# Split matmul operands of a fused graph block as pairs of float16 instead of 32-bit words

## The chip, the cores and the metric

The kernel runs on one core of one Trainium2 chip. The metric is the device time of one execution in microseconds (us); lower is better. TensorE does matmuls and transposes (the profile calls it PE, and its weight loads PEld), VectorE is DVE, ScalarE is ACT, GpSimd is POOL, and SP starts most of the DMAs.

## The reference

128 graphs of 128 nodes with 256 features each go through two stages. Stage L0 is a transformer block with 8 heads of 32 features and an adjacency bias; stage L1 is two rounds of single-head graph attention.

```python
# L0, for x of (128, 128, 256)
nx = ln(x); q, k, v = nx @ wq + bq, nx @ wk + bk, nx @ wv + bv       # 8 heads of 32
bias = where(adj > 0, 0.1 * adj * adj, -inf)
attn = softmax(q @ k.T / sqrt(32) + bias);  x1 = x + (attn @ v) @ wo + bo
x = x1 + gelu(ln(x1) @ w1 + b1) @ w2 + b2                             # 256 -> 1024 -> 256
# L1, for k in 0, 1
q, kk = x @ Wq[k].T + bq[k], x @ Wk[k].T + bk[k]                      # 256 -> 128
attn = softmax(where(adj == 0, -1e10, q @ kk.T / sqrt(128)))          # zero where masked
x = ln(x + (attn @ x) @ Wc[k].T) * g[k] + b[k]
```

## The kernel before

The 128 graphs are worked in 32 groups of 4, so that a group has 512 rows. All weights stay in SBUF. A matmul with a weight matrix needs more precision than one pass gives, so both operands are split in a high part (`_h`) and a low part (`_l`, the rest), and `mm3` makes three matmuls of one: high by high, high by low, low by high. Those are lines 244, 245 and 246 of the profile. The high part is made by ScalarE (it copies with a cast), the low part by VectorE (it subtracts the high part), and for the odd chunks of the hidden layer by GpSimd.

In this kernel the halves of the weights and of `xT`, `rot`, `hid` and `cT` (the transposed rows of each stage) are tiles of type float32r, 32-bit words that a matmul takes in one pass. The halves of q and k, of the softmax of L0 (`pT16`) and of v are float16 already. `to_columns` multiplies with a weight as the stationary operand and 512 rows as the moving one (128x512); `to_rows` and the `down` matmuls have 128 rows as the stationary operand and a weight of 256 columns as the moving one (128x256). Transposes, and the L1 scores and value products, are plain float32 and not part of the change.

Five lists of steps (`TENSOR`, `SCALAR`, `VECTOR`, `GPSIMD`, `SYNC`), written by hand, give the order of each engine's work in the steady loop; a step such as `M.down5-2` is chunk 5 of the second MLP product, two groups behind. Each engine does its list in order and waits by semaphores. One pass through the lists is one group. The step names that the prediction uses: `Q.k1` (a projection of L0), `C0.xW` (x times Wc in L1's first round, evicted by ScalarE to `cW`, then needed by `C0.PT` and `C0.PV`), `M.mT` and `M.up0` (transposes and first chunk of the MLP), `M.lo6` (low part of hidden chunk 6, on VectorE, from `split_hidden`, line 251), `C0.S`, `C1.S` (scores of L1).

The names of the profile are without digits: `w_h` is `w1_h` or `w2_h`, `area` is the scratch that holds scores, x1, x2, `cW` and the hidden layer.

Of the kernel before, what the change touches and what calls it, by code (L numbers as in the profile page):

```python
# [29 lines left out]
F32, F32R, F16, BF16, I32 = (mybir.dt.float32, mybir.dt.float32r, mybir.dt.float16,  # L30
                             mybir.dt.bfloat16, mybir.dt.int32)
ALU, ACT, AX = mybir.AluOpType, mybir.ActivationFunctionType, mybir.AxisListType

P = 128
# [12 lines left out]
RING = 3  # L47

# [28 lines left out]
def graph_blocks(nc, x, adj, ln1_g, ln1_b, ln2_g, ln2_b, wq, bq, wk, bk, wv, bv, wo, bo, w1, b1,  # L77
# [6 lines left out]
    with ExitStack() as ctx:  # L84
        def sb(name, shape, dt=F32):
            return ctx.enter_context(nc.sbuf_tensor(name, shape, dt))
# [7 lines left out]
        wqk_h, wqk_l = sb("wqk_h", [P, KC, 2 * D], F32R), sb("wqk_l", [P, KC, 2 * D], F32R)  # L94
        wv_h, wv_l = sb("wv_h", [P, KC, D], F32R), sb("wv_l", [P, KC, D], F32R)
        wo_h, wo_l = sb("wo_h", [P, KC, D], F32R), sb("wo_l", [P, KC, D], F32R)
        w1_h, w1_l = sb("w1_h", [P, KC, FF], F32R), sb("w1_l", [P, KC, FF], F32R)
        w2_h, w2_l = sb("w2_h", [P, FC, D], F32R), sb("w2_l", [P, FC, D], F32R)
        cqk_h, cqk_l = sb("cqk_h", [P, L, KC, 2 * P], F32R), sb("cqk_l", [P, L, KC, 2 * P], F32R)
        cw_h, cw_l = sb("cw_h", [P, L, KC, D], F32R), sb("cw_l", [P, L, KC, D], F32R)  # L100
# [6 lines left out]
        ln_q = sb("ln_q", [P, KC])  # L107
        cln_col = sb("cln_col", [P, 2, KC])
        cgq = sb("cgq", [P, KC])
# [22 lines left out]
        xT_h, xT_l = sb("xT_h", [P, KC, R], F32R), sb("xT_l", [P, KC, R], F32R)  # L132
# [6 lines left out]
        rot_h, rot_l = sb("rot_h", [P, KC, R], F32R), sb("rot_l", [P, KC, R], F32R)  # L139
        hid_h, hid_l = sb("hid_h", [P, RING, R], F32R), sb("hid_l", [P, RING, R], F32R)  # L140
        cT_h, cT_l = sb("cT_h", [P, KC, R], F32R), sb("cT_l", [P, KC, R], F32R)
# [227 lines left out]
        def _(pool):  # L369
# [3 lines left out]
            pool.memset(v_h[:, :, :, HD:VW], 1.0).then_inc(const_ok, 1)  # L373
# [75 lines left out]
        def _(act):  # L449

            act.wait_ge(prep_dve, 1)
# [14 lines left out]
            def iteration(it, odd):  # L466
                for stage, what, g in steps(SCALAR, it, odd):
# [79 lines left out]
        def _(dve):  # L547
            made = [0]

            def prep(instruction):  # L550
                made[0] += 1
                instruction.then_inc(prep_dve, 1)
# [4 lines left out]
            def lows(start, stop):  # L557

                for n in range(start, stop):
# [7 lines left out]
                    prep(dve.scalar_tensor_tensor(lo, raw, gain, hi.bitcast(F32), ALU.mult, ALU.subtract))  # L567
# [23 lines left out]
            prep(dve.tensor_scalar(ln_q[:, :], ln_col[:, 0, :], QSCALE, None, ALU.mult))  # L591
# [3 lines left out]
            prep(dve.tensor_scalar(cgq[:, :], cln_col[:, 0, :], CSCALE, None, ALU.mult))  # L595
# [29 lines left out]
            def iteration(it, odd):  # L625
                for stage, what, g in steps(VECTOR, it, odd):
                    b = int(what[-1]) if what[-1].isdigit() else None
                    if what == "mA":
# [7 lines left out]
                        dve.scalar_tensor_tensor(adj_f, adj_in[:, :, :], 0.1, adj_in[:, :, :],  # L636
# [16 lines left out]
                    elif stage == "N":  # L653
                        need(dve, a_xT, g, 1, 1)
                        dve.tensor_tensor(xT_l[:, :, :], psC, xT_h[:, :, :].bitcast(F32), ALU.subtract)\
# [21 lines left out]
                    elif stage == "A" and what[:3] == "max":  # L677
# [3 lines left out]
                        dve.tensor_scalar(nbias[:, b, :], nmax[:, b, :], -1.0, P_SCALE,  # L681
# [15 lines left out]
                    elif what == "oT":  # L697
                        need(dve, a_oT, g, 1, 1)
                        dve.tensor_tensor(rot_l[:, :, :], psA, rot_h[:, :, :].bitcast(F32), ALU.subtract)\
                           .then_inc(d_oT, 1)  # L700
                    elif what == "wo":
# [3 lines left out]
                        dve.tensor_tensor(x1, psA_rows, xin[:, g[1]], ALU.add).then_inc(d_x1, 1)  # L705
# [5 lines left out]
                    elif what == "mT":  # L711
                        need(dve, a_mT, g, 1, 1)
                        dve.tensor_tensor(rot_l[:, :, :], psM, rot_h[:, :, :].bitcast(F32), ALU.subtract)\  # L713
# [3 lines left out]
                    elif what == "x2":  # L717
# [424 lines left out]
```

## Time and profile before

| | us |
|---|---|
| median of three runs | 2311.23 |
| lowest, highest | 2309.97, 2317.95 |
| the profiled execution | 2311.21 |
| its span, first to last instruction | 2309.4 |

A row of the grouped view gives the line, engine and operation, what is written and read with the shapes, the number of instructions, then the busy time in us and the mean of one in ns, then the idle time of the engine just before them. A timeline row gives the start and the length in us. Matmuls are pipelined: the length of one is longer than its place in the stream, and the pace of a stream is the distance from one start to the next.

### The profile page before, as it was taken

What the parts mean: (1) busy time and instruction counts of PE and PEld (TensorE: products, weight loads), DVE (VectorE), ACT (ScalarE), POOL (GpSimd) and SP (SyncE); (2) the same over time, 40 slices, a digit from 0 to 9 for tenths busy, and PEclk for the clock granted to TensorE, in tenths of its full rate; (3) what the DMA queues carried; (4) which work ended last, traced back from release to release, by engine and by line L of the source; (5) the groups of instructions that cost most, each with busy time, mean ns of one, the idle gap of its engine ahead of it and who ended that gap; (6) DMA issues with size and microseconds to landing.
All of it is one profiled execution on the core that took longest, in us unless ns stands there. A gap on an engine that the chain in (4) does not pass through costs nothing.

```text
span 2309.4 us, 47435 instructions
## 1 busy us (share of the span) xinstructions
PE 2112.8 (91%) x16984; PEld 1898.2 (82%) x16984; DVE 1837.9 (80%) x3585; ACT 1566.9 (68%) x2994; POOL 874.1 (38%) x632
## 2 busy tenths in 40 slices
PE   5589999999999999999999999999999999999863
PEld 4578888888888888888888888898888888888752
DVE  3566788888888888888888888888888888887433
ACT  2367777777768776776787677777767777787421
POOL 2021343334444433343444333444433344444423
PEclk8799999999999999999999999999999999999985
DMA  3321112122221121222111122221111222210000
GB/s 100 71 53 34 39 36 51 47 56 56 56 57 42 29 53 45 56 56 56 46 39 42 42 56 56 56 56 43 35 49 43 56 56 55 56 47 15 15 10 18
DMA packets 103649, 108.61 MB, mean 47 GB/s; under 512 B 9824, under 2 KB 78432, under 8 KB 103456
## 3 DMA queue, kind: packets, MB, share of 16 engines
q1 hardware_dynamic: 102912, 104.90, 18.0%
q8 instruction: 163, 2.67, 0.5%
q0 software_dynamic: 544, 0.80, 0.2%
q14 instruction: 30, 0.25, 0.0%
HBM read 38.55 MB, written 16.78 MB: 24 GB/s over the span
## 4 chain that ended last, share of the span: by engine, by line
PE 76%; ACT 10%; DVE 9%; issue 3%; POOL 1%; DMA 0%; SPq 0%; POOLq 0%; DVEq 0%; ACTq 0%
PE ps L244 20%; PE ps L246 19%; PE ps L245 19%; PE ps L1114 5%; PE ps L816 5%; PE ps L1040 4%; PE ps L1094 3%; DVE hid_l L251 2%; ACT cs L530 2%; DVE rot_l L713 2%; ACT L530 2%; ACT area L538 1%; PE ps L1033 1%; ACT rot_h L502 1%; ACT ck L524 1%
## 5 line engine op out<-in xcount | busy, mean ns | idle before, releaser
L251 POOL TENSOR_TENSOR hid_l<-area,hid_h 128x512 fp32r<-128x512 f32 x128 | 165.4, 1292 | 721.2 <-ACT hid_h L512 721.2
L489 ACT ACTIVATE area<-area,nbias 128x128 f32<-128x128 f32 x1024 | 313.9, 392 | 1.0 <-DVE nbias L681 0.2
L244 PE MATMUL ps<-w_h,hid_h 128*128 128x256 f32 x1024 | 305.3, 298 | 3.2 <-POOL hid_l L251 1.8
L245 PE MATMUL ps<-w_l,hid_h 128*128 128x256 f32 x1024 | 286.2, 279 | 0.0
L246 PE MATMUL ps<-w_h,hid_l 128*128 128x256 f32 x1024 | 285.9, 279 | 0.0
L509 ACT ACTIVATE area<-ps,b_col 128x512 f32<-128x512 f32 x256 | 176.3, 689 | 118.3 <-PE ps L246 117.2
L244 PE MATMUL ps<-rot_h,w_h 128*128 128x512 f32 x512 | 215.3, 420 | 11.6 <-DVE rot_l L713 10.8
L674 DVE TENSOR_TENSOR area<-ps,biasA 128x1024 f32<-128x1024 f32 x128 | 155.8, 1218 | 79.4 <-PE ps L1033 77.6
L246 PE MATMUL ps<-rot_h,w_l 128*128 128x512 f32 x512 | 202.2, 395 | 0.0
L245 PE MATMUL ps<-rot_l,w_h 128*128 128x512 f32 x512 | 202.0, 395 | 0.0
L244 PEld LDWEIGHTS ps<-w_h,hid_h 128*128 128x128 f32 x1024 | 193.1, 189 | 7.9 <-POOL hid_l L251 2.2
L245 PEld LDWEIGHTS ps<-w_l,hid_h 128*128 128x128 f32 x1024 | 194.0, 189 | 3.7
L246 PEld LDWEIGHTS ps<-w_h,hid_l 128*128 128x128 f32 x1024 | 193.0, 188 | 0.0
L403 POOL TENSOR_TENSOR ve<-mv,eps_cols 128x4 f32<-128x4 f32 x128 | 26.9, 210 | 422.5 <-DVE mv L577 421.8
L524 ACT ACTIVATE cq<-ps,cb_col 128x512 f32<-128x512 f32 x64 | 43.9, 686 | 206.9 <-PE ps L246 206.9
L512 ACT CAST hid_h<-area 128x512 fp32r<-128x512 f32 x256 | 159.1, 621 | 8.1
L685 DVE TENSOR_TENSOR pT<-ps,pT 128x1024 f16<-128x1024 f32 x128 | 155.6, 1216 | 11.1 <-ACT pT L495 9.5
L415 POOL TENSOR_TENSOR x<-x,cb_row 128x1024 f32<-128x1024 f32 x64 | 161.8, 2527 | 5.0
L426 POOL TENSOR_TENSOR area<-area,cwb_row 128x1024 f32<-128x1024 f32 x32 | 76.3, 2383 | 221.8 <-ACT area L538 221.8
L679 DVE TENSOR_REDUCE nmax<-area 128x8 f32<-128x1024 f32 x128 | 155.4, 1214 | 1.1
L816 PE MATMUL ps<-ident,area 128*128 128x128 f32 x1024 | 135.4, 276 | 21.4 <-DVE area L585 18.7
L244 PE MATMUL ps<-cw_h,cT_h 128*128 128x256 f32 x512 | 146.9, 287 | 5.5 <-DVE cs L733 5.5
(176 smaller groups left out, 6952.3 us busy)
## 6 DMA issues: line engine op xcount, KB each, us to landing
qkS<-qk SPq DMA_DIRECT2D x384, 128.0 KB, 2.4
xin<-in_x SPq DMA_DIRECT2D x32, 512.0 KB, 4.0
adj_in<-in_adj SPq DMA_DIRECT2D x64, 256.0 KB, 4.0
out<-x SPq DMA_DIRECT2D x32, 512.0 KB, 3.3
area<-in_L_gnn_w SPq DMA_DIRECT2D x2, 1024.0 KB, 11.9
area<-in_L_gnn_Wc SPq DMA_DIRECT2D x2, 256.0 KB, 11.9
area<-in_L_gnn_wq SPq DMA_DIRECT2D x1, 256.0 KB, 3.5
area<-in_L_gnn_wk SPq DMA_DIRECT2D x1, 256.0 KB, 4.4
```

Source lines behind the costliest of these rows:

```text
L244: pe.matmul(dst, lh, rh, start=start, stop=False, **kw)
L245: pe.matmul(dst, lh, rl, start=False, stop=False, **kw)
L246: return pe.matmul(dst, ll, rh, start=False, stop=stop, **kw)
L251: eng.tensor_tensor(hid_l[:, c % RING, :], hidden[:, c % 2, :], hid_h[:, c % RING, :].bitcast(F32), ALU.subtract).then_inc(done, 1)
L415: pool.tensor_tensor(dst, dst, over_graphs(cb_row[:, l, :]), ALU.add).then_inc(p_c[l], 1)
L489: last = act.activation(sc[:, b % 2, h], sc[:, b % 2, h], ACT.Exp, bias=nbias[:, b, h:h + 1])
L509: act.activation(hidden[:, b % 2, :], psUp, ACT.Gelu, bias=b1_col[:, b:b + 1]).then_inc(a_gelu, 1)
L512: act.copy(hid_h[:, b % RING, :], hidden[:, b % 2, :]).then_inc(a_hi, 1)
L674: dve.tensor_tensor(sc[:, b % 2], psA_heads, biasA[:, b].unsqueeze(1).broadcast_to([P, H, P]), ALU.add).then_inc(d_S, 1)
L679: dve.tensor_reduce(nmax[:, b, :], sc[:, b % 2], AX.X, ALU.max).then_inc(d_max, 1)
L685: dve.tensor_tensor(pT16[:, b % 2, 1], psA_heads, pT16[:, b % 2, 0], ALU.subtract)\
L816: last = pe.transpose(dst[:, c, b * P:(b + 1) * P], rows[:, b, c * P:(c + 1) * P], ident[:, :])
```

## The change

All split tiles become float16. High parts are then rounded to float16, low parts are the float16 of what is left. So that the low parts of weights don't fall below the range of float16, weights are multiplied by 256 when they are split, and the places that read a product from PSUM divide by 256 (q and k of L0 stay scaled; their scores are divided by 65536 inside the exponential, and the bias is multiplied by it). The ones column of v, from which the sum of the softmax comes, is 256 too, so that the division by it removes the factor of v.

```diff
-        w2_h, w2_l = sb("w2_h", [P, FC, D], F32R), sb("w2_l", [P, FC, D], F32R)
+        w2_h, w2_l = sb("w2_h", [P, FC, D], F16), sb("w2_l", [P, FC, D], F16)
...                       (wqk, wv, wo, w1, cqk, cw, xT, rot, hid, cT alike)
-            pool.memset(v_h[:, :, :, HD:VW], 1.0).then_inc(const_ok, 1)
+            pool.memset(v_h[:, :, :, HD:VW], W_SCALE).then_inc(const_ok, 1)
...
-            act.wait_ge(prep_dve, 1)
+            act.wait_ge(prep_dve, 3)
...
                             last = act.activation(sc[:, b % 2, h], sc[:, b % 2, h], ACT.Exp,
-                                                  bias=nbias[:, b, h:h + 1])
+                                                  bias=nbias[:, b, h:h + 1], scale=1.0 / QK_SCALE)
...
                         act.activation(hidden[:, b % 2, :], psUp, ACT.Gelu,
-                                       bias=b1_col[:, b:b + 1]).then_inc(a_gelu, 1)
+                                       bias=b1_col[:, b:b + 1], scale=1.0 / W_SCALE).then_inc(a_gelu, 1)
...
                             act.activation((cq, ck)[i][:, :], psC[:, i, :], ACT.Identity,
-                                           bias=cb_col[:, i, l:l + 1]).then_inc((a_cq, a_ck)[i][l], 1)
+                                           bias=cb_col[:, i, l:l + 1],
+                                           scale=1.0 / W_SCALE).then_inc((a_cq, a_ck)[i][l], 1)
...
-                            act.copy(cW, psC_rows).then_inc(a_cW[l], 1)
+                            act.activation(cW, psC_rows, ACT.Copy, scale=1.0 / W_SCALE).then_inc(a_cW[l], 1)
...
-            prep(dve.tensor_scalar(ln_q[:, :], ln_col[:, 0, :], QSCALE, None, ALU.mult))
+            prep(dve.tensor_scalar(ln_q[:, :], ln_col[:, 0, :], QSCALE * W_SCALE, None, ALU.mult))
+            prep(dve.tensor_scalar(ln_kv[:, 0, :], ln_col[:, 0, :], W_SCALE, None, ALU.mult))
+            prep(dve.tensor_scalar(ln_kv[:, 1, :], ln_col[:, 2, :], W_SCALE, None, ALU.mult))
...
-                        dve.tensor_scalar(nbias[:, b, :], nmax[:, b, :], -1.0, P_SCALE,
+                        dve.tensor_scalar(nbias[:, b, :], nmax[:, b, :], -1.0 / QK_SCALE, P_SCALE,
...
-                        dve.tensor_tensor(x1, psA_rows, xin[:, g[1]], ALU.add).then_inc(d_x1, 1)
+                        dve.scalar_tensor_tensor(x1, psA_rows, 1.0 / W_SCALE, xin[:, g[1]],
+                                                 ALU.mult, ALU.add).then_inc(d_x1, 1)
...
-                        dve.tensor_tensor(x2, psM_rows, x1, ALU.add).then_inc(d_x2, 1)
+                        dve.scalar_tensor_tensor(x2, psM_rows, 1.0 / W_SCALE, x1,
+                                                 ALU.mult, ALU.add).then_inc(d_x2, 1)
```

Four small VectorE instructions are added in the preparation ahead of the first group. In the loop no instruction is added, removed or moved on any engine: the sequences are the same, and in 64 places each a `COPY` of ScalarE (`cW`) becomes an `ACTIVATE`, and a `TENSOR_TENSOR` of VectorE (`x1`, `x2`) a `SCALAR_TENSOR_TENSOR`. No DMA changes, since the weights are still loaded as float32 and split on the chip.

## Rows read from the trace of the kernel before

**Rows 1.** The page: busy time by engine; granted TensorE clock, tenths, 40 slices

```profile
PE 2112.8 (91%) x16984; PEld 1898.2 (82%) x16984; DVE 1837.9 (80%) x3585; ACT 1566.9 (68%) x2994; POOL 874.1 (38%) x632
...
PEclk8799999999999999999999999999999999999985
```

**Rows 2.** A stretch: length, PE, PEld, DVE, ACT, POOL busy, clock, DMA share, GB/s

```profile
948.00:1596.00 648.00, 623.99 (x5093) 563.80 (x5093) 557.33 (x1091) 472.47 (x902) 262.78 (x187) 1.00 0.19 47
```

**Rows 3.** Waits of PE from 300 to 2100: us in total, times, longest

```profile
PE ps L244 <- issue: 16.5, 10, 2.0
PE ps L1105 <- ACT area L538: 14.6, 28, 0.6
PE ps L1094 <- ACT ck L524: 11.0, 27, 0.4
PE ps L244 <- DVE qk L660: 9.0, 13, 0.9
```

**Rows 4.** Timeline, DVE: start, length; the same step of two successive groups

```profile
1181.59 1.22 DVE L674 TENSOR_TENSOR area<-ps,biasA 128x1024 f32<-128x1024 f32 x1 [3.10 <-PE ps L1033]
...
1247.49 1.23 DVE L674 TENSOR_TENSOR area<-ps,biasA 128x1024 f32<-128x1024 f32 x1 [1.39 <-PE ps L1033]
```

**Rows 5.** The chain that ended last, from 300 to 2100, shares by line

```profile
by line: PE ps L244 21.8%; PE ps L246 20.6%; PE ps L245 20.5%; PE ps L816 5.3%; PE ps L1114 5.3%; PE ps L1040 4.1%; PE ps L1094 3.0%; DVE hid_l L251 2.6%; issue 2.4%; ACT cs L530 2.2%; ACT L530 2.0%; DVE rot_l L713 1.9%; ACT rot_h L502 1.4%
```

**Rows 6.** Timeline, PE: three streams of 24 matmuls, first of each and what follows

```profile
1186.50 0.40 PE L244 MATMUL ps<-rot_h,w_h 128*128 128x512 f32 x1
...
1192.09 1.05 PE L1094 MATMUL ps<-ck,cq 128*128 128x128 f32 x8
...
1215.35 0.28 PE L244 MATMUL ps<-wo_h,rot_h 128*128 128x256 f32 x1
...
1218.17 0.40 PE L244 MATMUL ps<-cT_h,cqk_h 128*128 128x512 f32 x1
...
1224.31 0.28 PE L244 MATMUL ps<-cw_h,cT_h 128*128 128x256 f32 x1
...
1227.03 1.04 PE L816 MATMUL ps<-ident,area 128*128 128x128 f32 x8
```

**Rows 7.** Timeline, PE: eight float16 matmuls, then a float32r product starts

```profile
1246.83 0.62 PE L1033 MATMUL ps<-qkS 96*128 96x128 f16 x8
1247.26 0.48 PE L244 MATMUL ps<-rot_h,w_h 128*128 128x512 f32 x1
1247.58 0.40 PE L245 MATMUL ps<-rot_l,w_h 128*128 128x512 f32 x1
```

**Rows 8.** Groups by line and form: matmuls of two products (first of three each)

```profile
L244 PE MATMUL ps<-w_h,hid_h 128*128 128x256 f32 x1024 | 305.3, 298 | 3.2 <-POOL hid_l L251 1.8 <-DVE hid_l L251 1.3
...
L244 PE MATMUL ps<-rot_h,w_h 128*128 128x512 f32 x512 | 215.3, 420 | 11.6 <-DVE rot_l L713 10.8 <-ACT area L509 0.8
```

**Rows 9.** Groups by line and form: weight loads of 32-bit and of float16 operands

```profile
L246 PEld LDWEIGHTS ps<-w_h,hid_l 128*128 128x128 f32 x1024 | 193.0, 188 | 0.0
...
L246 PEld LDWEIGHTS ps<-v_h,pT 128*128 128x128 f16 x1024 | 79.6, 96 | 0.0
```

**Rows 10.** Groups by form: a PSUM tile read in two ways on ACT and DVE

```profile
L478 ACT ACTIVATE qk<-ps,bqk_col 128x512 f16<-128x512 f32 x128 | 88.0, 687 | 40.0 <-PE ps L246 39.7
...
L483 ACT CAST v_h<-ps 128x512 f16<-128x512 f32 x64 | 37.2, 581 | 116.7 <-PE ps L246 116.7
...
L660 DVE SCALAR_TENSOR_TENSOR qk<-ps,bqk_col,qk 128x512 f16<-128x512 f32 x128 | 95.4, 745 | 51.0 <-ACT qk L478 51.0
...
L665 DVE TENSOR_TENSOR v_l<-ps,v_h 128x512 f16<-128x512 f32 x64 | 42.9, 671 | 0.0
```

**Rows 11.** Low parts of the hidden layer on VectorE: the group, then one (timeline)

```profile
L251 DVE TENSOR_TENSOR hid_l<-area,hid_h 128x512 fp32r<-128x512 f32 x128 | 121.5, 949 | 19.3 <-ACT hid_h L512 19.3
...
1200.48 2.30 DVE L251 TENSOR_TENSOR hid_l<-area,hid_h 128x512 fp32r<-128x512 f32 x1
```

**Rows 12.** Timeline, POOL, the same time

```profile
1199.85 2.38 POOL L413 TENSOR_TENSOR x<-xh,cg_row 128x1024 f32<-128x1024 f32 x1 [1.73 <-DMA out<-x]
```

More of the change, by code:

```diff
@@ L28 @@
 from concourse import mybir
-F32, F32R, F16, BF16, I32 = (mybir.dt.float32, mybir.dt.float32r, mybir.dt.float16,
-                             mybir.dt.bfloat16, mybir.dt.int32)
+F32, F16, BF16, I32 = mybir.dt.float32, mybir.dt.float16, mybir.dt.bfloat16, mybir.dt.int32
 ALU, ACT, AX = mybir.AluOpType, mybir.ActivationFunctionType, mybir.AxisListType
@@ L47 @@
 RING = 3
+W_SCALE = 256.0
+QK_SCALE = W_SCALE * W_SCALE
 TENSOR = ["Q.k0+0", "M.down2-2", "A.S2-1", "M.up4-2", "C0.q-3", "A.PT1-1", "M.down3-2", "M.up5-2",
@@ L92, in graph_blocks @@
         ident = sb("ident", [P, P])
[L94 to L97, printed above, removed]
-        w2_h, w2_l = sb("w2_h", [P, FC, D], F32R), sb("w2_l", [P, FC, D], F32R)
-        cqk_h, cqk_l = sb("cqk_h", [P, L, KC, 2 * P], F32R), sb("cqk_l", [P, L, KC, 2 * P], F32R)
-        cw_h, cw_l = sb("cw_h", [P, L, KC, D], F32R), sb("cw_l", [P, L, KC, D], F32R)
+        wqk_h, wqk_l = sb("wqk_h", [P, KC, 2 * D], F16), sb("wqk_l", [P, KC, 2 * D], F16)
+        wv_h, wv_l = sb("wv_h", [P, KC, D], F16), sb("wv_l", [P, KC, D], F16)
+        wo_h, wo_l = sb("wo_h", [P, KC, D], F16), sb("wo_l", [P, KC, D], F16)
+        w1_h, w1_l = sb("w1_h", [P, KC, FF], F16), sb("w1_l", [P, KC, FF], F16)
+        w2_h, w2_l = sb("w2_h", [P, FC, D], F16), sb("w2_l", [P, FC, D], F16)
+        cqk_h, cqk_l = sb("cqk_h", [P, L, KC, 2 * P], F16), sb("cqk_l", [P, L, KC, 2 * P], F16)
+        cw_h, cw_l = sb("cw_h", [P, L, KC, D], F16), sb("cw_l", [P, L, KC, D], F16)
         ln_col = sb("ln_col", [P, 4, KC])
@@ L106, in graph_blocks @@
         cb_col = sb("cb_col", [P, 2, L])
-        ln_q = sb("ln_q", [P, KC])
+        ln_q, ln_kv = sb("ln_q", [P, KC]), sb("ln_kv", [P, 2, KC])
         cln_col = sb("cln_col", [P, 2, KC])
-        cgq = sb("cgq", [P, KC])
+        cgq, cgk = sb("cgq", [P, KC]), sb("cgk", [P, KC])
         bo_row, b2_row = sb("bo_row", [P, D]), sb("b2_row", [P, D])
@@ L131, in graph_blocks @@
         xin = sb("xin", [P, 2, B, D])
[L132 removed]
+        xT_h, xT_l = sb("xT_h", [P, KC, R], F16), sb("xT_l", [P, KC, R], F16)
         qk16 = sb("qk16", [P, 4, 2, R], F16)
@@ L138, in graph_blocks @@
         v_h, v_l = sb("v_h", [P, B, H, VW], F16), sb("v_l", [P, B, H, VW], F16)
-        rot_h, rot_l = sb("rot_h", [P, KC, R], F32R), sb("rot_l", [P, KC, R], F32R)
-        hid_h, hid_l = sb("hid_h", [P, RING, R], F32R), sb("hid_l", [P, RING, R], F32R)
-        cT_h, cT_l = sb("cT_h", [P, KC, R], F32R), sb("cT_l", [P, KC, R], F32R)
+        rot_h, rot_l = sb("rot_h", [P, KC, R], F16), sb("rot_l", [P, KC, R], F16)
+        hid_h, hid_l = sb("hid_h", [P, RING, R], F16), sb("hid_l", [P, RING, R], F16)
+        cT_h, cT_l = sb("cT_h", [P, KC, R], F16), sb("cT_l", [P, KC, R], F16)
         cq, ck = sb("cq", [P, R]), sb("ck", [P, R])
@@ L287, in graph_blocks @@
             halves += [(wqk_h[:, c, 0:D], wqk_l[:, c, 0:D], raw_qkvo[:, 0, c], ln_q[:, c:c + 1]),
-                       (wqk_h[:, c, D:2 * D], wqk_l[:, c, D:2 * D], raw_qkvo[:, 1, c], ln_col[:, 0, c:c + 1]),
-                       (wv_h[:, c], wv_l[:, c], raw_qkvo[:, 2, c], ln_col[:, 0, c:c + 1])]
-        halves += [(wo_h[:, :, :], wo_l[:, :, :], raw_qkvo[:, 3], 1.0)]
+                       (wqk_h[:, c, D:2 * D], wqk_l[:, c, D:2 * D], raw_qkvo[:, 1, c], ln_kv[:, 0, c:c + 1]),
+                       (wv_h[:, c], wv_l[:, c], raw_qkvo[:, 2, c], ln_kv[:, 0, c:c + 1])]
+        halves += [(wo_h[:, :, :], wo_l[:, :, :], raw_qkvo[:, 3], W_SCALE)]
         HALVES_QKVO = len(halves)
         for c in range(KC):
-            halves += [(w1_h[:, c], w1_l[:, c], raw_w1[:, c], ln_col[:, 2, c:c + 1])]
+            halves += [(w1_h[:, c], w1_l[:, c], raw_w1[:, c], ln_kv[:, 1, c:c + 1])]
         HALVES_W1 = len(halves)
-        halves += [(cqk_h[:, 0, :, 0:P], cqk_l[:, 0, :, 0:P], layer_qk[0][:, 0], CSCALE),
-                   (cqk_h[:, 0, :, P:2 * P], cqk_l[:, 0, :, P:2 * P], layer_qk[0][:, 1], 1.0),
-                   (cw_h[:, 0], cw_l[:, 0], layer_w[0], 1.0)]
+        halves += [(cqk_h[:, 0, :, 0:P], cqk_l[:, 0, :, 0:P], layer_qk[0][:, 0], CSCALE * W_SCALE),
+                   (cqk_h[:, 0, :, P:2 * P], cqk_l[:, 0, :, P:2 * P], layer_qk[0][:, 1], W_SCALE),
+                   (cw_h[:, 0], cw_l[:, 0], layer_w[0], W_SCALE)]
         HALVES_C0 = len(halves)
         for c in range(KC):
-            gain = cln_col[:, 0, c:c + 1]
+            gain = cgk[:, c:c + 1]
             halves += [(cqk_h[:, 1, c, 0:P], cqk_l[:, 1, c, 0:P], layer_qk[1][:, 0, c], cgq[:, c:c + 1]),
@@ L304, in graph_blocks @@
         HALVES_L1 = len(halves)
-        halves += [(w2_h[:, :, :], w2_l[:, :, :], raw_w2, 1.0)]
-        PREP_DVE = 14 + len(halves)
-        BV_MADE = 1 + HALVES_W1 + 6
+        halves += [(w2_h[:, :, :], w2_l[:, :, :], raw_w2, W_SCALE)]
+        PREP_DVE = 18 + len(halves)
+        BV_MADE = 3 + HALVES_W1 + 8
         L1_COPIED = BV_MADE + 3
@@ L566, in lows @@
                     dve.wait_ge(prep_act, made)
-                    prep(dve.scalar_tensor_tensor(lo, raw, gain, hi.bitcast(F32), ALU.mult, ALU.subtract))
+                    prep(dve.scalar_tensor_tensor(lo, raw, gain, hi, ALU.mult, ALU.subtract))
             def stats(g, n, rows):
@@ L600, in _ @@
             prepped()
-            prep(dve.tensor_scalar(bqk_col[:, 0:2], bqk_col[:, 0:2], QSCALE, None, ALU.mult))
+            prep(dve.tensor_scalar(bqk_col[:, 0:2], bqk_col[:, 0:2], QSCALE * W_SCALE, None, ALU.mult))
+            prep(dve.tensor_scalar(bqk_col[:, 2:4], bqk_col[:, 2:4], W_SCALE, None, ALU.mult))
             prep(dve.tensor_copy(bv_rep, bv_col[:, :].unsqueeze(2).broadcast_to([P, KC, P])))
-            assert made[0] == BV_MADE
+            assert made[0] == BV_MADE, made[0]
             dve.wait_ge(prep_pe, 2)
@@ L698, in iteration @@
                         need(dve, a_oT, g, 1, 1)
-                        dve.tensor_tensor(rot_l[:, :, :], psA, rot_h[:, :, :].bitcast(F32), ALU.subtract)\
+                        dve.tensor_tensor(rot_l[:, :, :], psA, rot_h[:, :, :], ALU.subtract)\
                            .then_inc(d_oT, 1)
@@ L712, in iteration @@
                         need(dve, a_mT, g, 1, 1)
-                        dve.tensor_tensor(rot_l[:, :, :], psM, rot_h[:, :, :].bitcast(F32), ALU.subtract)\
+                        dve.tensor_tensor(rot_l[:, :, :], psM, rot_h[:, :, :], ALU.subtract)\
                            .then_inc(d_mT, 1)
```

11 lines of the change are left out of this document (6 added, 5 removed).

## The prediction

> **What bounds the kernel now.** I read the page first. PE is busy 91% of the span and DVE 80% [rows 1]; the length of one matmul overlaps the next, so 91% doesn't yet say that PE is the bound. A stretch of the steady loop has PE busy 624 of 648 us and DVE 557, at the full clock of 2.4 GHz [rows 2]. The waits say the rest: from 300 to 2100 us PE waits at four places for the sum of 51 us, 3% [rows 3], and everything else is its own stream. The same step of two successive groups starts 65.9 us apart [rows 4]: that is the period, and 32 groups with the filling and the draining make the span. The chain of that stretch is 62.9% on lines 244 to 246, the three matmuls of a split product, another 18% on other PE lines, and some 19% on ACT, DVE and issue [rows 5]. So PE's pace sets the time, but not alone: a fifth of the chain is latency of the engines that evict and split.
>
> **The pace of a split matmul.** A stream's pace is start to start. Twenty-four float32r matmuls of 512 columns take 5.59 us, 233 ns each; 24 of `wo` with 256 columns take 2.82 us, 117.5 ns; 24 of `cw` take 2.72 us, 113.3 ns [rows 6]. Eight float16 matmuls of 128 columns take 0.43 us, 54 ns each [rows 7]. At 2.4 GHz one column per cycle would be 213, 107 and 53 ns. So the float16 stream runs at about a column per cycle and the float32r ones 6 to 10% slower, at two sizes in proportion, which looks like a cost per column and not per instruction. What I take for float16: 216 ns and 108 ns, four times and twice the 54 of rows 7. The saving is 17, 9.5 and 5.3 ns. Bounds: nothing, if the slow pace comes from adding into PSUM, which the eight of rows 7 do not do; and at most 20, 11 and 7 ns, down to a column per cycle.
>
> Per group there are 96 matmuls of 512 columns (a third of each line's 512 plus 256 plus 256 over 32 groups: `rot` with w1 512 [rows 8], and `xT` and `cT` 256 each by the code), 120 of 256 columns in `down` and `wo` (1024 [rows 8] and 256 per line), and 72 in `xW` and `v` (512 and 256 per line). That is 96 x 17 + 120 x 9.5 + 72 x 5.3 ns = 1.63 + 1.14 + 0.38 = 3.15 us.
>
> **The weight load at the start of a run.** A load takes 188 ns with 32-bit words and 96 ns with float16 [rows 9]. Within a stream it hides under the matmul before; after a short one it can't. The first float32r matmul behind the eight float16 ones holds the stream 0.32 us instead of 0.23 [rows 7], while those eight, which follow a float32r product themselves, show no such excess in their mean of 54. The list `TENSOR` goes from another kind of matmul into a split product 14 times per group. At 0.09 us, less the shorter load, all 14 would give 1.2 us; a few start behind a wait, where some of it is hidden, so I take 0.9 us. Zero is not possible here unless a float16 load of these tiles is slower than that of `pT`.
>
> The Trainium skill (TensorE: Matmul & The Clock Gate, Weight-path perf modes) has a fast weight load for 128 columns of a type that is not FP32, which agrees with 96 against 188. The same section says that the array takes one element per cell and cycle whatever the element's width: by that rule the 3.15 us would be nothing, and only the 0.9 left. The rows speak against it, since 233 is not four times 54; it is the second rival.
>
> **What the edits cost.** `cW` goes from a copy to an activation. On a PSUM tile of 512 columns an activation takes 687 ns and a cast 581 [rows 10]: 0.1 us more, twice per group. One of the two, `C0.xW`, is what PE waits for at L1105 in each group (28 times [rows 3]): 32 x 0.106 = 3.4 us on the path. The other feeds GpSimd's `cWb`, with no wait of PE behind it in rows 3: nothing. `x1` and `x2` become three-operand instructions: 745 against 671 ns [rows 10], 0.07 us twice per group at most, 4.7 us in all. DVE has 14% idle [rows 2] which hides part; queued behind `x1` are the statistics, for which `M.mT` waits. I take 1.5 us. The exponential, gelu and q and k change a constant only. A cast that writes float16 costs what one into float32r does as far as rows go: nothing. The four small instructions of the preparation run while weights are still on their way. GpSimd's subtraction with a float16 input has no row; nothing is what I take, and up to some tenths of a us stay hidden unless PE waits for its chunk, which it doesn't in rows 3. Sum of costs: 5 us.
>
> **What arrives at the end.** PE's own work falls by 3.15 + 0.9 = 4.05 us a group, 130 us over 32 groups, 5.6%. Not all of it can show:
> - The split matmuls are 96 x 0.233 + 120 x 0.1175 + 72 x 0.113 + 1.2 = 45.8 us of 65.9, 69% of the time. On the chain the three lines have 62.9%; about 4% of it are the float16 products of v, between 96 x 14 ns and 96 x 54 ns by columns or by instruction from rows 7. So 59 of 69 parts are on the chain: 130 x 0.85 = 111 us.
> - Where PE waits for ACT or DVE, their latency doesn't shrink, and PE now comes earlier. The order of the lists is fixed for the old durations, and DVE is busy 86% of the steady loop [rows 2]; with 4 us less it would be 92%. Late next, after the four places of rows 3, are the low parts that PE needs soonest: `rot_l` and `hid_l` (1.9% and 2.6% of the chain already [rows 5]). I choose to give a quarter of the rest to such new waits: 83 us.
> - The first 300 and last 200 us are latency more than stream (the granted clock is 8 and 7 tenths in the first two slices and 5 in the last [rows 1]); some 5 us go there. That leaves 78.
>
> 78 less 5 is 73 us: 2311.2 (the profiled execution, which is the median within 0.1 us) less 73 is 2238.
>
> **Rivals.**
> 1. *Nothing is lost.* ACT and DVE move forward with PE, because most of their idle time is waiting for PE. Then 130 less 5: 2186. For it: DVE's 86% of 65.9 us [rows 2, 4] are 57 us, still under a period of 62. Against: the 19% of other engines on the chain. Between this and the forecast lies a continuum; I take it as up to 2205. Chance 0.13.
> 2. *Width doesn't set the pace*; the 6 to 10% come from the accumulation or another cause that float16 keeps. Then 0.9 us x 32 = 29, of which 85% and three quarters remain, 18, less 5: 2298. Chance 0.17.
> 3. *The other engines take it all*: the loop through DVE's in-order list is already nearly as long as PE's, so the new waits eat nearly everything: 2300 to 2315. Against it: PE waits 3% only, so what it waits for is mostly early. Chance 0.07.
> 4. *Slower, by a collision.* One `hid_l` of VectorE per group takes 2.30 us where the mean is 949 ns and the rest 0.7 [rows 11]; at that time GpSimd runs an addition of 2.38 us [rows 12], and the two instructions with two SBUF inputs seem not to run together. There are four such `hid_l` a group. If the shorter times shift more of them under GpSimd's long ones, each costs 1.6 us x 32 = 51 us of DVE and, at the head of a `down`, of PE. One more eats two thirds of the gain, two more turn it: 2238 + 102 = 2340. Nothing shows that the shift, some 4 us over a period, would pick the wrong direction; one that leaves would be a gain. Chance 0.05.
>
> The rest, 0.58, is the forecast with 2205 to 2290 as its own range.
>
> **How the numbers follow.** A difference under 0.5% (12 us) can't be told from none here. Faster by more is the forecast, the first rival, and most of the second where it reaches below 2299.7 (0.6 of 0.17), together 0.83. Same: the rest of the second and most of the third, 0.11. Slower: 0.06, from the fourth and a little of the third. The range reaches from the first rival's near half to the second's middle: 2192 to 2298.
>
> **What the profile after would show.** Streams of 512 columns with starts 216 ns apart and of 256 with 108 (the second rival: still 233 and 113 to 118). Weight loads of all split products at 96 ns; the step behind the eight score matmuls at 0.23 or less instead of 0.32. The period under 65.9 us, near 63.7. PE waits at L1105, L1094, `rot_l` and `Q.k1` longer than the 51 us of now, by 20 to 40 us. `cW` on ACT at 1.1 us. The forecast would be wrong by the pace (an unshown type at these sizes), or by how many waits come through, which I set by judgement; the sign would be wrong only by a lengthened DVE, which the mean of its `hid_l` would tell.

## The result, and the profile after

The changed kernel takes 2274.38 us (2272.66 to 2277.72, four runs), the kernel before 2310.6 us (2309.05 to 2317.95, four runs) on the same chip: a ratio of 0.9849, 95% interval 0.9828 to 0.987. The gain is 36 us where 73 were forecast. The time lies inside the range of 2192 to 2298, but half of the expected gain is missing, so the working of the prediction has a step that failed, and the question of the experiments is which. The profiled execution took 2277.72 us with a span of 2275.9.

The page after: busy time by engine, and the chain that ended last by engine.

```profile
PE 2026.2 (89%) x16984; PEld 1512.2 (66%) x16984; DVE 1887.3 (83%) x3589; ACT 1562.6 (69%) x2994; POOL 845.8 (37%) x632
...
PE 56%; DVE 21%; ACT 13%; issue 7%; POOL 1%; DMA 0%; SPq 0%; DVEq 0%; POOLq 0%; ACTq 0%
```

Against [rows 1] PE's busy time falls by 87 us and that of its weight loads by 386 us. VectorE's *rises* by 49 us, although its instructions are the same but for 64 and four small ones. That is the first thing to explain. The window of 648 us (columns as in [rows 2]) says the same of the steady loop: VectorE goes from 557 to 575 us, and PE drops to 608 of 648, so it now waits for longer.

```profile
948.00:1596.00 648.00, 607.59 (x5215) 456.65 (x5213) 575.41 (x1092) 480.15 (x920) 260.02 (x188) 0.99 0.19 49
```

The waits of PE from 300 to 2100, after:

```profile
PE ps L245 <- DVE qk L666: 47.8, 27, 2.3
PE ps L245 <- issue: 19.4, 10, 2.2
PE ps L1113 <- ACT area L540: 17.1, 27, 0.7
PE ps L1102 <- ACT ck L525: 11.4, 27, 0.4
PE ps L245 <- DVE rot_l L720: 7.6, 27, 0.3
```

In [rows 3] four places sum to 51 us, and with the 6.3 us for `rot_l`, which is the next in that view, to 57; the same five sum to 103 here. Of these 46 us more, 39 are at one place, `Q.k1`, which waits for q or k of VectorE (9.0 before, 47.8 now).

The pace of PE's streams, by the same reading as [rows 6]:

```profile
1171.33 0.38 PE L245 MATMUL ps<-rot_h,w_h 128*128 128x512 f16 x1
...
1176.51 1.05 PE L1102 MATMUL ps<-ck,cq 128*128 128x128 f32 x8
...
1178.71 0.61 PE L1041 MATMUL ps<-qkS 96*128 96x128 f16 x8
1179.16 0.27 PE L245 MATMUL ps<-cw_h,cT_h 128*128 128x256 f16 x1
1179.27 0.27 PE L246 MATMUL ps<-cw_l,cT_h 128*128 128x256 f16 x1
...
1181.78 0.38 PE L245 MATMUL ps<-xT_h,wqk_h 128*128 128x512 f16 x1
```

Twenty-four matmuls of 512 columns take 5.18 us, 216 ns each instead of 233; 24 of `cw` take 2.62 us, 109 ns instead of 113.3. Note that the length of one (0.38, 0.27) says nothing of the pace. From the first of the eight score matmuls to the first of `cw`, and on to the second, it is 0.45 + 0.11 us; the same entry takes 0.43 + 0.20 in the kernel before (medians of 27 groups).

Last, what VectorE and GpSimd do when PE waits at `Q.k1` (three timelines: VectorE, PE, GpSimd).

```profile
1179.14 1.18 DVE L746 TENSOR_SCALAR cmax<-cneg 128x4 f32<-128x4 f32 x1
...
1184.54 2.47 DVE L252 TENSOR_TENSOR hid_l<-area,hid_h 128x512 f16<-128x512 f32 x1
1186.93 0.74 DVE L666 SCALAR_TENSOR_TENSOR qk<-ps,bqk_col,qk 128x512 f16<-128x512 f32 x1
```

```profile
1187.73 0.39 PE L245 MATMUL ps<-xT_h,wqk_h 128*128 128x512 f16 x1 [1.07 <-DVE qk L666]
```

```profile
1177.93 2.36 POOL L416 TENSOR_TENSOR x<-x,cb_row 128x1024 f32<-128x1024 f32 x1
...
1184.10 2.36 POOL L414 TENSOR_TENSOR x<-xh,cg_row 128x1024 f32<-128x1024 f32 x1 [1.50 <-DMA out<-x]
```

`hid_l` starts 0.44 us after a GpSimd multiplication and ends 0.55 us after that one's end at 1186.46. This `hid_l` is the step `M.lo6`. VectorE's part of the eviction of q (`Q.q1`, L666) is queued behind it and begins only then, and PE's next projection behind that. `cmax`, an instruction over 4 elements per partition, takes 1.18 us and ends at 1180.32, when GpSimd's addition ends (1180.29).

The groups of VectorE in which its time grew, and the weight load; after, then before (the row of `hid_l` of before is in [rows 11], of the load in [rows 9]).

```profile
L252 DVE TENSOR_TENSOR hid_l<-area,hid_h 128x512 f16<-128x512 f32 x128 | 137.7, 1076 | 21.7 <-ACT hid_h L513 20.5
L587 DVE TENSOR_SCALAR xh<-xh,mv,rs 128x256 f32<-128x256 f32 x128 | 67.4, 589 | 0.7 <-POOL rs L406 0.7
L746 DVE TENSOR_SCALAR cmax<-cneg 128x4 f32<-128x4 f32 x64 | 60.1, 939 | 2.2
L687 DVE TENSOR_SCALAR nbias<-nmax 128x8 f32<-128x8 f32 x128 | 45.0, 351 | 4.4
L247 PEld LDWEIGHTS ps<-w_h,hid_l 128*128 128x128 f16 x1024 | 100.1, 98 | 11.6
```

```profile
L585 DVE TENSOR_SCALAR xh<-xh,mv,rs 128x256 f32<-128x256 f32 x128 | 52.1, 470 | 0.7 <-POOL rs L405 0.7
L738 DVE TENSOR_SCALAR cmax<-cneg 128x4 f32<-128x4 f32 x64 | 37.5, 585 | 2.2
L681 DVE TENSOR_SCALAR nbias<-nmax 128x8 f32<-128x8 f32 x128 | 31.7, 247 | 4.4
```

The excess is 127 ns x 128 + 119 x 128 + 354 x 64 + 104 x 128 = 67 us, 2.1 us per group. Nothing in these four but the types of `hid_l`'s operands and the factor of `nbias` was changed.

The collision itself is not new. Only one `hid_l` of the four in a group is stretched, in both kernels: `M.lo6` takes over 1.5 us in 27 of its 32 groups before and in 28 after, and its mean goes from 1.74 to 2.25 us, while the other three stay at 0.68 to 0.69. So `M.lo6` doesn't stand under GpSimd's pass more often now, it meets it earlier and stands there longer.

### The profile page after: what moved, and what is told of

Its sections match the earlier page's. It is cut to its first block, busy times and chain, and to the rows that moved or that the text cites. A ratio compares the mean times of both kernels' runs of the same rounds, so it can differ in the third digit from the quotient of the medians.

```text
span 2275.9 us, 47439 instructions
## 1 busy us (share of the span) xinstructions
PE 2026.2 (89%) x16984; PEld 1512.2 (66%) x16984; DVE 1887.3 (83%) x3589; ACT 1562.6 (69%) x2994; POOL 845.8 (37%) x632
## 4 chain that ended last, share of the span: by engine, by line
PE 56%; DVE 21%; ACT 13%; issue 7%; POOL 1%; DMA 0%; SPq 0%; DVEq 0%; POOLq 0%; ACTq 0%
PE ps L245 13%; PE ps L247 13%; PE ps L246 13%; PE ps L824 5%; PE ps L1122 5%; PE ps L1048 3%; DVE hid_l L252 3%; DVE nmax L685 3%; ACT area L490 3%; DVE xh L587 2%; PE ps L1102 2%; DVE rot_l L720 2%; DVE qk L666 2%; DVE st L574 1%; ACT L490 1%
## 5 line engine op out<-in xcount | busy, mean ns | idle before, releaser
L252 POOL TENSOR_TENSOR hid_l<-area,hid_h 128x512 f16<-128x512 f32 x128 | 148.7, 1162 | 748.7 <-ACT hid_h L513 748.7
L245 PE MATMUL ps<-w_h,hid_h 128*128 128x256 f16 x1024 | 279.0, 272 | 2.7 <-DVE hid_l L252 1.6
L247 PE MATMUL ps<-w_h,hid_l 128*128 128x256 f16 x1024 | 279.1, 273 | 0.0
L246 PE MATMUL ps<-w_l,hid_h 128*128 128x256 f16 x1024 | 279.1, 273 | 0.0
L680 DVE TENSOR_TENSOR area<-ps,biasA 128x1024 f32<-128x1024 f32 x128 | 155.6, 1216 | 66.1 <-PE ps L1041 66.0
L245 PE MATMUL ps<-rot_h,w_h 128*128 128x512 f16 x512 | 195.0, 381 | 12.7 <-DVE rot_l L720 11.2
L246 PE MATMUL ps<-rot_l,w_h 128*128 128x512 f16 x512 | 194.7, 380 | 0.0
L247 PE MATMUL ps<-rot_h,w_l 128*128 128x512 f16 x512 | 194.7, 380 | 0.0
L513 ACT CAST hid_h<-area 128x512 f16<-128x512 f32 x256 | 158.3, 618 | 8.2
L824 PE MATMUL ps<-ident,area 128*128 128x128 f32 x1024 | 136.7, 277 | 21.9 <-DVE area L587 19.1
L252 DVE TENSOR_TENSOR hid_l<-area,hid_h 128x512 f16<-128x512 f32 x128 | 137.7, 1076 | 21.7 <-ACT hid_h L513 20.5
L1048 PE MATMUL ps<-ident,area 128*128 128x128 f32 x1024 | 138.5, 280 | 11.3 <-ACT area L490 7.0
L245 PE MATMUL ps<-cw_h,cT_h 128*128 128x256 f16 x512 | 141.0, 275 | 6.1 <-DVE cs L741 6.1
```

The costliest lines, as they stand in the source:

```text
L245: pe.matmul(dst, lh, rh, start=start, stop=False, **kw)
L246: pe.matmul(dst, lh, rl, start=False, stop=False, **kw)
L247: return pe.matmul(dst, ll, rh, start=False, stop=stop, **kw)
L680: dve.tensor_tensor(sc[:, b % 2], psA_heads, biasA[:, b].unsqueeze(1).broadcast_to([P, H, P]), ALU.add).then_inc(d_S, 1)
L824: last = pe.transpose(dst[:, c, b * P:(b + 1) * P], rows[:, b, c * P:(c + 1) * P], ident[:, :])
L1048: last = pe.transpose(psA_heads[:, h], sc[:, b % 2, h], ident[:, :])
```

## The experiments

Theory A: the pace and nothing else gives the gain, about 94 us from the streams above, and the rest of it is eaten because VectorE's instructions from SBUF to SBUF now stand longer under GpSimd's 2.4 us instructions. Theory B: the gain is lost to latency that doesn't shrink, as the prediction had it, or to the edits themselves. Eleven kernels ran, named by what they change. Beside them the kernel before was measured again, with medians of 2310.2 to 2311.6 us, so that their times can be set against the two above.

**1 and 2. A light GpSimd, in both kernels.** The passes that multiply by the gain, add the bias, and add b2 to x1 work on 16 of 256 columns; the same in the changed kernel (first) and in the kernel before (second). Everything else stays in place and order; what these passes would do to the other 240 columns is left out.

```diff
-pool.tensor_tensor(dst, src, over_graphs(cg_row[:, l, :]), ALU.mult).then_inc(p_cg[l], 1)
+pool.tensor_tensor(dst[:, :, 0:16], src[:, :, 0:16], over_graphs(cg_row[:, l, :])[:, :, 0:16], ALU.mult).then_inc(p_cg[l], 1)
...                 (the addition of cb_row, and that of b2_row to x1, alike)
```

> The changed kernel, but GpSimd's two affine passes after each norm of L1 and its addition to x1 work on 16 columns of a graph's 256 instead of all (the outputs lack the gain and bias of the rest). Theory A (the gain was eaten because VectorE instructions on SBUF operands now stand under GpSimd's 2.4 us passes: hid_l 1076 ns mean, cmax 939, xh 589): these go back to 0.69, 0.17 and 0.41 us, and the time falls from 2274 to about 2225. Rival B (the port is innocent; the fixed latency of ScalarE and VectorE in order holds the period): 2262 to 2274.

> The same cut of GpSimd's passes in the kernel before. Theory A: its collisions cost less (hid_l 949 ns, cmax 585), so 2311 falls to about 2290, and the ratio of the two light kernels is 0.970 to 0.975, near what was forecast, instead of 0.985. Rival B: 2300 to 2311 and a ratio still 0.985.

Measured: 2195.99 us (0.9499, 0.9474 to 0.9524) with the change, 2283.35 us (0.9871, 0.9845 to 0.9897) without. Between these two the change is worth 87 us, a ratio of 0.962, where it is worth 36 in the full kernels. Both times are lower than either expectation had them (about 2225 and 2290, ratio 0.970 to 0.975). The light kernel also drains sooner, which is part of that: behind the last step of L1's bias (`biasC`) on VectorE 87 us are left instead of 99 without the change, and 81 instead of 95 with it; in the pair this cancels to 2 us. What is left of the effect of GpSimd's passes on the loop is 27 - 12 = 15 us in the kernel before and 78 - 14 = 64 us in the changed one. The light changed kernel, window, waits and groups:

```profile
948.00:1596.00 648.00, 624.41 (x5402) 470.64 (x5401) 558.18 (x1130) 495.96 (x959) 160.58 (x196) 1.00 0.19 51
```

```profile
PE ps L245 <- issue: 19.0, 10, 2.2
PE ps L1113 <- ACT area L540: 17.4, 28, 0.7
PE ps L1102 <- ACT ck L525: 12.2, 28, 0.9
PE ps L245 <- DVE rot_l L720: 9.1, 28, 1.6
```

```profile
L252 DVE TENSOR_TENSOR hid_l<-area,hid_h 128x512 f16<-128x512 f32 x128 | 87.4, 683 | 22.4 <-ACT hid_h L513 21.4
...
L746 DVE TENSOR_SCALAR cmax<-cneg 128x4 f32<-128x4 f32 x64 | 11.3, 177 | 2.2
```

and the group of the light kernel before:

```profile
L251 DVE TENSOR_TENSOR hid_l<-area,hid_h 128x512 fp32r<-128x512 f32 x128 | 87.4, 683 | 18.1 <-ACT hid_h L512 18.1
```

Writing float16 costs `hid_l` nothing (683 ns in both), `cmax` takes 177 ns, and the wait at `Q.k1` is gone. The waits that stay are 58 us here, and 65 with the small ones that the view lists below these; the light kernel before has 49 and 50 by the same count. So A holds, and of the latency that the prediction feared, 15 us in 1800 are to be seen. Light passes also end sooner, which could help whoever waits for GpSimd; the next experiments leave them at full length.

**3 and 4. One step of VectorE later, in both kernels.** `M.lo6` changes places with the q eviction that PE waited for behind it.

```diff
-"A.AV0-1", "M.lo6-2", "Q.q1+0",
+"A.AV0-1", "Q.q1+0", "M.lo6-2",
```

> The changed kernel with two neighbours of VectorE's list exchanged: the subtraction of Q.q1 ahead of M.lo6, which needs nothing of it. Theory A: PE's wait at Q.k1 for that subtraction (1.8 us per group, behind a hid_l of 2.5 us) disappears, 2274 becomes about 2235. Rival B (the wait only moves to the next low part or softmax step): above 2265.

> The same exchange in the kernel before, where the wait is 0.3 us per group. Theory A: 2311 falls by 5 to 12 us. Rival B: no change within 3 us. With e3 it tells whether the changed kernel alone is bound there.

Measured: 2239.56 us (0.9684, 0.966 to 0.9708) after, 2296.68 us (0.9933, 0.9904 to 0.9962) before. The swap gives 35 us with the change, 4 short of the first expectation, and 14 without, a little over the 5 to 12 expected; the pair is 57 us apart. The wait behind q is gone, but another, as the second expectation had it, stands in its place, for the softmax that is queued behind `M.lo6` now:

```profile
PE ps L1048 <- DVE pT L691: 15.6, 17, 1.0
```

**5. The factors alone.** The scaled kernel with all tiles left as 32-bit words.

```diff
-        w2_h, w2_l = sb("w2_h", [P, FC, D], F16), sb("w2_l", [P, FC, D], F16)
+        w2_h, w2_l = sb("w2_h", [P, FC, D], F32R), sb("w2_l", [P, FC, D], F32R)
...                 (all split tiles alike; the factors stay)
```

> Only the other half of the change: weights times 256, the evictions and the softmax with their factors, cW by an activation, x1 and x2 by three-operand instructions, but all split tiles still float32r. Theory A (the profile after has cW at 1007 ns for 998 and x1, x2 at 1225 for 1225): no change, 2308 to 2316 beside 2311. Rival B (my 5 us of costs): 2316 or more.

Measured: 2311.84 us against 2310.53, ratio 1.0002 (0.9986 to 1.0018). Groups of that kernel: `cW` on ScalarE, then x2 and x1 on VectorE.

```profile
L541 ACT ACTIVATE area<-ps 128x1024 f32<-128x1024 f32 x64 | 64.6, 1010 | 6.0 <-PE ps L248 6.0
...
L729 DVE SCALAR_TENSOR_TENSOR area<-ps,area 128x1024 f32<-128x1024 f32 x32 | 39.2, 1225 | 4.7 <-PE ps L248 0.5
L712 DVE SCALAR_TENSOR_TENSOR area<-ps,xin 128x1024 f32<-128x1024 f32 x32 | 39.2, 1224 | 17.2 <-PE ps L248 17.2
```

The copy took 998 ns in the kernel before, and x1 as a plain addition 1224. In sum the edits cost nothing that can be measured, and the whole change of time comes with the type of the operands. The sum hides two shifts. With the factors, products on 32-bit words run slower: summed start to start over 24 groups they take 0.7 us per group more (one of `cw` 119 ns instead of 113, medians), though nothing in these matmuls but the values and the place of the tiles differs. And PE's waits from 300 to 2100 us are 46 us instead of 58. Why is open; the float16 streams, with the same factors, run at 109 ns.

**6 and 10. The type of some products alone,** with the light GpSimd so that no collision blurs it: only `hid` and w2 (the `down` matmuls) as float16; then only `rot`, w1 and wo.

```diff
-        w2_h, w2_l = sb("w2_h", [P, FC, D], F32R), sb("w2_l", [P, FC, D], F32R)
+        w2_h, w2_l = sb("w2_h", [P, FC, D], F16), sb("w2_l", [P, FC, D], F16)
...                 (hid_h, hid_l alike; in the other kernel rot, w1 and wo instead)
```

> GpSimd's passes light as in the light kernels, scaling as in the change, and float16 only for the hidden layer and w2 (the down product, 96 matmuls of 256 columns per group, entered six times from another kind of matmul); the rest stays float32r (outputs lack gain and bias as before). Beside 2283 of the light kernel with words. Theory A (only the pace pays, an entry pays only behind a float16 block, which down has once per group): 0.8 to 0.9 us per group, 2255 to 2260. Rival B (each of the entries pays 0.075 us, as the prediction counted): 1.25 us per group, 2240 to 2246.

> As e6, but float16 for rot, w1 and wo only (48 matmuls of 512 columns and 24 of 256 per group), beside 2283 of the light kernel with words. Theory A (the pace alone: 48 x 17 + 24 x 8.5 ns = 1.0 us per group): 2248 to 2254. Rival B (entries pay as the prediction counted): 2235 to 2242.

Measured: 2263.19 us (0.98, 0.9768 to 0.9832) for `down`, 2262.1 us (0.979, 0.9773 to 0.9808) for `rot`, w1 and wo; against the light kernel before 20 us and 21 us. By pace alone I would work out 96 x 8.4 ns x 32 = 26 us and (48 x 17.1 + 24 x 8.4) ns x 32 = 33 us. Both expectations on the first asked for more than was found, the one with a gain at the start of each run above all. On the second both expected a larger gain than the 21 us. The remaining products then hold 87 - 41 = 46 us, where the pace gives 36.

The parts can't be read so finely, because the light kernel before has no factors and these two have: the products that stay on words run slower here too. Summed start to start over 24 groups they take 0.6 us per group more in the first of the two and 1.2 us in the second than in the light kernel before, 19 and 39 us in 32 groups. That is more than the 6 and 12 us that are missing; shorter waits and other steps give part of it back. So these two kernels neither confirm nor refute the pace of a single product, and by themselves they don't refute the gain at the starts either; the entries are read from the traces below.

**7 and 8. The low part later still, in both kernels.** `M.lo6` goes behind the softmax and value steps too.

```diff
-"A.AV0-1", "M.lo6-2", "Q.q1+0", "A.PT2-1", "A.AV1-1", "Q.k1+0"
+"A.AV0-1", "Q.q1+0", "A.PT2-1", "A.AV1-1", "M.lo6-2", "Q.k1+0"
```

> The changed kernel with M.lo6 later in VectorE's list: behind A.AV1, where VectorE waits anyway, and where GpSimd's second pass of C0.af is nearly over; the subtraction of Q.q1 and the softmax step A.PT2 go ahead of it. Theory A (VectorE's list ahead of Q.k1 holds the period, and hid_l costs 2.5 us only beside that pass): both the wait and the collision go, 2205 to 2225. Rival B (the wait of PE moves to the low part itself or to PT3): 2235 or above, as the simple exchange gave.

> The same move in the kernel before. Theory A: 2285 to 2295, since its wait there was 0.3 us per group. Ratio of the two late kernels 0.965 to 0.972, near that of the light pair (0.962). Rival B: ratio 0.975 or above, as for the simple exchange.

Measured: 2221.05 us (0.9604, 0.9588 to 0.962) after, 2292.88 us (0.9913, 0.9895 to 0.993) before. This is a full kernel and the fastest of the full ones: 90 us under the kernel before and 53 under the changed one. The same move gives 18 us without the change. The pair is 72 us apart. Its `hid_l` and `cmax`:

```profile
L252 DVE TENSOR_TENSOR hid_l<-area,hid_h 128x512 f16<-128x512 f32 x128 | 101.1, 790 | 21.8 <-ACT hid_h L513 20.2
...
L746 DVE TENSOR_SCALAR cmax<-cneg 128x4 f32<-128x4 f32 x64 | 60.1, 938 | 2.2
```

`hid_l` is down from 1076 ns, `cmax` is as long as in the changed kernel, and no wait of PE in the view is put down to it: a stretched instruction matters where PE's next operand is queued behind it. Both times are as the first expectation had them, the ratio of the pair too (0.969). Of the 25 us that this kernel is behind the light one, 14 are draining; the other 11 are in no wait that the view lists.

**9. One GpSimd pass light.** Only the gain and bias of `C0.af`, the pass under which `M.lo6` stands, on 16 columns.

```diff
-affine(g, 0, x3[:, :, :], xh3[:, :, :])
+affine(g, 0, x3[:, :, 0:16], xh3[:, :, 0:16])
...                 (the rows of the gain and the bias are cut to the width of dst)
```

> The changed kernel with only C0.af light (GpSimd's two passes beside M.lo6 on 16 of 256 columns; the other passes full). Theory A (the collision that reaches PE is that of the one hid_l with C0.af; those of xh, nbias and cmax lie ahead of it and delay VectorE's list too): hid_l falls to 0.69 us everywhere, the wait at Q.k1 by most of its 1.8 us, and the time to 2215 to 2235. Rival B (it is the earlier collisions with C1.af and x1b, which this leaves in): above 2250.

Measured: 2226.52 us (0.9631, 0.961 to 0.9651), inside the first expectation: 48 us of the 78 that all the passes give, or of the 64 without the draining, which this kernel does not shorten (97 us behind the last `biasC`). Mean of `hid_l` 709 ns, and the wait at `Q.k1`:

```profile
PE ps L245 <- DVE qk L666: 5.1, 17, 0.4
```

So one pair of steps per group, GpSimd's `C0.af` (two passes) and VectorE's `M.lo6`, is most of what is missing.

**11. A GpSimd step moved instead.** The late kernel, with `x1b` behind `C0.af`, to take it off `cmax`.

```diff
-"C1.af-4", "A.x1b-1", "C0.af-3", "M.lo7-1"
+"C1.af-4", "C0.af-3", "M.lo7-1", "A.x1b-1"
```

> The late kernel of e7, and GpSimd's addition A.x1b moved behind M.lo7, where GpSimd is idle, so that cmax of C0.max no longer stands under it. Theory A: cmax falls from 938 to some 200 ns mean, VectorE is 1 to 2 us per group less busy and PE no longer waits for it: 2205 to 2218. Rival B (after e7 PE waits only for ScalarE and rot_l, none of which this touches): 2218 to 2224.

Measured: 2240.6 us (0.9693, 0.9674 to 0.9713): 20 us slower than the late kernel, and outside of both expectations. Groups and waits of that kernel, then `nbias` (VectorE) and a GpSimd multiplication in the timeline:

```profile
L687 DVE TENSOR_SCALAR nbias<-nmax 128x8 f32<-128x8 f32 x128 | 60.2, 471 | 4.4
L746 DVE TENSOR_SCALAR cmax<-cneg 128x4 f32<-128x4 f32 x64 | 22.5, 351 | 2.2
```

```profile
PE ps L245 <- DVE rot_l L720: 28.3, 29, 1.6
...
PE ps L245 <- DVE cs L741: 8.7, 28, 0.8
```

```profile
1230.33 2.36 DVE L687 TENSOR_SCALAR nbias<-nmax 128x8 f32<-128x8 f32 x1
```

```profile
1230.30 2.36 POOL L414 TENSOR_TENSOR x<-xh,cg_row 128x1024 f32<-128x1024 f32 x1 [3.30 <-DMA out<-x]
```

`cmax` was freed as meant (938 to 351 ns), but the passes that follow moved under `nbias`, for which the exponential waits, and `rot_l` came later (9.1 to 28.3 us in 1800). How much of the 20 us is the collision and how much is the later `x1b`, which x2 needs, stays open.

## Why the prediction was half right, by its own steps

- **The pace** (3.15 us per group). Right: 216 and 108 ns were taken, 216 and 109 measured, and loads of 98 ns. With the measured steps it is 96 x 17.1 + 120 x 8.4 + 72 x 4.2 ns = 2.95 us, 94 us over 32 groups. This is still a little high, since the 233 ns of [rows 6] hold the longer first step of that stream, which the prediction counts again as an entry. By medians of all steps from 300 to 2100 us the words take 231 to 232 ns (512 columns), 117 (`down`), 118 (`wo`) and 113 to 114 (`cw`, `wv`), which gives 2.8 us per group, 89 us. The second rival (width doesn't set the pace) falls.
- **The weight load at the start of a run** (0.9 us per group, 29 us). This step failed: it is the term that was mis-sized. It was read from one place behind float16 scores and taken for all 14. Ten of the 14 start behind float32 matmuls (seven times transposes), and nothing is gained there. The same entry, transposes to `down`, in the kernel before and after:

```profile
1184.21 1.03 PE L1040 MATMUL ps<-ident,area 128*128 128x128 f32 x8
1185.00 0.36 PE L244 MATMUL ps<-w_h,hid_h 128*128 128x256 f32 x1
1185.20 0.28 PE L245 MATMUL ps<-w_l,hid_h 128*128 128x256 f32 x1
```

```profile
1183.68 1.07 PE L1048 MATMUL ps<-ident,area 128*128 128x128 f32 x8
1184.59 0.27 PE L245 MATMUL ps<-w_h,hid_h 128*128 128x256 f16 x1
1184.70 0.27 PE L246 MATMUL ps<-w_l,hid_h 128*128 128x256 f16 x1
```

  It was 0.79 + 0.20 = 0.99 us and is 0.91 + 0.11 = 1.02, by the medians of 54 and 56 such entries 1.01 both times: the second matmul comes sooner, the last transpose holds the stream longer. Behind float16 matmuls there is a gain at four places per group. Behind the scores it is 0.43 + 0.20 to 0.45 + 0.11 for `cw` and 0.43 + 0.32 to 0.45 + 0.22 for `rot`; behind the value products the step from the first to the second split matmul goes from 0.20 to 0.11 for `down` and from 0.32 to 0.22 for `Q.k1` (in the light kernels, where no wait blurs it). Less the pace this is 0.06 to 0.09 us each, 0.3 us per group where 0.9 were taken, 10 us in all instead of 29.
- **The cost of the edits** (5 us). Nothing, by the run with the factors alone; a bound from tiles of 512 columns and another operation did not carry over to 1024 columns, where the copy already takes 998 ns and the activation 1010.
- **The share on the chain** (0.85) **and the quarter lost to new waits.** Pace and entries as measured are 89 + 10 = 99 us. Without the collisions 87 of them arrive, and 15 us of new waits account for what doesn't, within 3 us. So nine tenths arrive where the prediction let less than two thirds through (83 of 130): both deductions were too large for a kernel without collisions. The first rival's reason is right, ScalarE and VectorE move forward with PE; its 2186 took the entries at their full size and left out the collisions.
- **The new waits** (28 us). This is the step that failed most: the sum left VectorE's instructions as long as they were and put their collisions with GpSimd at nothing. The loss to them is 87 - 36 = 51 us, beside the 15 us of latency that stays when PE gets faster. It is the mechanism of the fourth rival, which had a chance of 0.05: VectorE's instructions under GpSimd's. I took it for a risk that only `hid_l` runs, by one more `hid_l` of a group being caught, and wrote that nothing shows the direction of the shift. No further `hid_l` was caught; the one that was caught already stands 0.5 us longer, and with three other kinds of instruction VectorE takes 2.1 us per group more. The part in `M.lo6` is in front of the eviction of q. Light GpSimd, one light pass, and the low part moved show it three ways: 78, 48 and 53 us of the changed kernel come back, the first with 14 us of draining in it. In the kernel before, all passes and the move give 27 and 18 us. After the move the change is worth 72 us, not 87; the last 15 us are put down to GpSimd's passes by the light kernels alone.
- **What the profile after would show.** The pace, the loads, the step behind the scores (0.22 us) and the wait at `Q.k1` came as written. L1105 and L1094 did not grow much (14.6 to 17.1 and 11.0 to 11.4), `cW` is at 1007 ns instead of 1.1 us, and the mean distance of one step over 24 groups is 65.5 us instead of 63.7; by the same count it was 66.3 before ([rows 4] show one pair of groups). It is 63.2 in the light changed kernel. PE's waits grew by 46 us, over the 20 to 40. The line on the mean of `hid_l` was the right one to watch: 1076 for 949 ns.
- **Slips that change little.** GpSimd's instruction in [rows 12] is the multiplication by the gain (L413), not an addition. The chances for faster sum to 0.58 + 0.13 + 0.10 = 0.81, not 0.83. The errors in the sum are 31 us too much for pace and entries (130 for 99), 45 us too much taken off for other reasons (57 for 12), and 51 us of collisions at nothing. The first two partly cancel, and that, with the width of the range, is why the time still lies in it: luck, not the working.

So the account is: 99 us by pace and entries, 87 to be seen where nothing collides, 51 of them taken by VectorE standing behind GpSimd, 36 left.

## What to carry to other kernels

When one engine gets faster, the order of two others against each other shifts; look in the timeline for instructions that are stretched by a neighbour (one of 0.2 us that takes 2.4), and for what is queued behind them, before giving a chance to "the waits will take a quarter". A stretched instruction is cheap to move behind an eviction that PE needs and worth it in both kernels, but count it again after the change: the move gave 18 us before and 53 after. Read a gain per entry at each kind of entry, since behind one neighbour it is real and behind another it only moves within the same microsecond.

## What the runs showed of the hardware

- A VectorE `TENSOR_SCALAR` of 4 or 8 elements per partition from SBUF to SBUF (`cmax`, `nbias`) takes up to 2.36 us while GpSimd runs a `TENSOR_TENSOR` of 512 or 1024 elements per partition, and 0.17 us otherwise; it ends 0.03 us after GpSimd's. `hid_l`, with two SBUF inputs, ends 0.55 us after it (both medians, whatever the wait was). Instructions that read PSUM (L666 at 0.74 us, L680 at 1.21 us) and `TENSOR_REDUCE` (1.22 us) keep their length beside it, and beside GpSimd's instruction of 4 elements (L406, 1.05 us) `hid_l` keeps its 0.69 us too. The Trainium skill (SBUF — State Buffer, "SBUF: two separate sides") says that VectorE in a two-port mode, or with two SBUF inputs, and GpSimd take a shared pair of ports as an exclusive lock, and the loser is fully blocked. The traces agree but for that small instruction of GpSimd, beside which `hid_l` isn't held. They show that an instruction over 8 elements pays as much as one over 512: `nbias` in experiment 11 takes all of 2.36 us.
- A stream of float16 matmuls takes 216 ns at 512 columns and 109 at 256, one of 32-bit words 231 to 233 and 113 to 118 (up to 119 to 120 in the kernels with factors), at a granted clock of 0.99 to 1.00 in the windows. The Trainium skill (TensorE: Matmul & The Clock Gate, "Back-to-back issue gap") has N/2.4 + 2.5 ns, 216 and 109: the traces agree for float16, and measure 4 to 10% more for the words.
- Making the input of GpSimd's subtraction float16 shortens it from 1292 to 1162 ns (128x512, 128 times; 1291 and 1162 in the light pair): a cost that the prediction had left at nothing is a small gain.
